# Input rows in their own buffer, five unequal loads, and low parts of the values spread over two row tiles

## The reference

```
scores = where(adj > 0, x @ weight @ input.T, -2**32 + 1)       # 6144 x 6144
atten  = softmax(scores / 0.07, axis=1)
x      = layernorm(x + atten @ input)
# second layer
Wh     = x @ W ;  s1 = Wh @ a1 ;  s2 = Wh @ a2
e      = leaky_relu(s1[:, None] + s2[None, :], 0.2)
att    = softmax(where(adj > 0, e, -9e15), axis=1)
out    = layernorm(x + elu(att @ Wh))
```

## Time and profile before

| | us |
|---|---|
| median of 3 runs | 1605.18 |
| lowest and highest | 1605.13, 1605.41 |
| profiled execution | 1605.25 |
| its span in the trace | 1603.3 |

### The profile page before, as it was taken

The page is one execution under the profiler, slowest core; times in us unless marked ns, Lnnn a source line. Parts: engine busy times, 40 slices in busy tenths (PEclk is TensorE's granted clock), DMA queues, the critical chain, the costliest instruction groups (busy, mean ns, idle before and its releaser), DMA issues.

```text
span 1603.3 us, 29354 instructions
## 1 busy us (share of the span) xinstructions
PE 1520.6 (95%) x10380; PEld 1088.5 (68%) x10380; DVE 1393.5 (87%) x2425; ACT 1061.9 (66%) x2396; POOL 833.3 (52%) x550
## 2 busy tenths in 40 slices
PE   7799999999999999999999999959999999999993
PEld 3577777777777777777777777755665656565652
DVE  6999999999999999999999999957778787888872
ACT  3577777777777777777777777766544444344433
POOL 5343333444343343344433433318988887878784
PEclk9999999999999999999999999989999999999997
DMA  7655555556555555555555555343344333434310
GB/s 236 221 176 187 180 186 199 204 204 204 192 193 180 181 183 197 204 205 204 200 188 185 182 181 191 122 81 79 79 79 92 79 76 81 87 79 92 80 33 13
DMA packets 228208, 241.11 MB, mean 150 GB/s; under 512 B 157152, under 2 KB 203488, under 8 KB 228064
## 3 DMA queue, kind: packets, MB, share of 16 engines
q1 hardware_dynamic: 228064, 239.25, 48.1%
HBM read 160.56 MB, written 40.89 MB: 126 GB/s over the span
## 4 chain that ended last, share of the span: by engine, by line
PE 85%; POOL 4%; issue 3%; DVE 3%; ACT 2%; POOLq 0%; ACTq 0%; DVEq 0%
PE ps L494 16%; PE ps L470 15%; PE ps L558 11%; PE ps L551 8%; PE ps L472 8%; PE ps L507 7%; PE ps L506 7%; PE ps L505 7%; PE ps L535 4%; POOL p_lo L396 2%; DVE p L866 1%; POOL m_w L401 1%; PE ps L567 1%; ACT p_hi L680 1%; DVE ve L907 1%
## 5 line engine op out<-in xcount | busy, mean ns | idle before, releaser
L645 ACT CAST pT_hi<-ps 128x512 f16<-128x512 f32 x576 | 335.8, 583 | 176.3 <-PE ps L494 173.1
L651 ACT ACTIVATE rows<-rows,exp_bias 128x512 f32<-128x512 f32 x576 | 417.9, 725 | 38.5 <-DVE exp_bias L841 38.5
L470 PE MATMUL ps<-vals,pT_hi 128*128 128x256 f16 x2304 | 442.0, 273 | 0.9 <-ACT att L639 0.8
L349 POOL TENSOR_SCALAR edges<-neg_mask 128x1536 uint8<-128x1536 bf16 x192 | 284.3, 1481 | 294.2 <-DVE neg_mask L755 290.3
L866 DVE SCALAR_TENSOR_TENSOR p<-ps,e_col,edgesT 128x1024 f32<-128x1024 f32 x288 | 353.9, 1277 | 87.7 <-POOL p_lo L396 50.4
L396 POOL TENSOR_TENSOR p_lo<-p,p_hi 128x1024 fp32r<-128x1024 f32 x156 | 369.6, 2382 | 80.2 <-PE ps L535 59.9
L472 PE MATMUL ps<-vals,pT_lo 128*128 128x128 f16 x2304 | 411.2, 219 | 0.0
L778 DVE CUSTOM_DVE_ANT_0 rows<-ps,neg_mask 128x1024 f32<-128x1024 f32 x288 | 351.8, 1222 | 52.5 <-PE ps L507 48.7
L787 DVE TENSOR_TENSOR pT_lo<-ps,pT_hi 128x512 f16<-128x512 f32 x576 | 389.3, 683 | 6.5 <-ACT pT_hi L645 6.4
L494 PE MATMUL ps<-ident,rows 128*128 128x128 f32 x2304 | 350.9, 275 | 3.4 <-DVE pT_lo L787 3.2
L680 ACT CAST p_hi<-p 128x1024 fp32r<-128x1024 f32 x156 | 162.9, 1048 | 245.8 <-DVE p L866 241.5
(11 more groups left out here) (99 smaller groups left out, 1323.9 us busy)
## 6 DMA issues: line engine op xcount, KB each, us to landing
adj_sb<-adj SPq DMA_DIRECT2D x192, 768.0 KB, 6.2
edge_rows<-edges SPq DMA_DIRECT2D x192, 192.0 KB, 5.1
rows<-inp SPq DMA_DIRECT2D x4, 768.0 KB, 9.6
xq<-x SPq DMA_DIRECT2D x48, 64.0 KB, 2.0
xr<-x SPq DMA_DIRECT2D x48, 64.0 KB, 1.8
out<-y_w SPq DMA_DIRECT2D x6, 512.0 KB, 3.6
edgesT<-edge_rows SPq DMA_TRANSPOSE x48, 5.3
x_all<-w SPq DMA_DIRECT2D x1, 64.0 KB, 1.8
```

What stands on the lines that cost most here:

```text
L470: nc.tensor.matmul(acc, pT_hi[:, s, cols], vals[:, jb, :], start=(jb == 0), stop=False, skip_group_check=True)
L645: nc.scalar.copy(pT_hi[:, bc % PT_SLOTS, :], ps[:, PT0 + bc % NPT, :]).then_inc(pT_hi_set, 1)
L651: nc.scalar.activation(row_chunk(1 - par, c), row_chunk(1 - par, c), ACT.Exp, bias=exp_bias[:, 1 - par:2 - par], scale=EXP_SCALE, accum_ou ...
```

## The change

It has four parts.

- The input rows get a buffer of their own, `inp_sb`, of 24 KB in each partition. `rows` holds masked scores and turned input chunks only.
- They are loaded in five transfers of 4, 8, 12, 12 and 12 row blocks. The load of x stands behind the first of them, and each later one is followed by a quarter of the adjacency. GpSimd's high parts follow the same five pieces.
- `vals_low` leaves its place in steps 0 to 11 of tile 0, and with it goes the wait of VectorE on itself. Chunks 0 to 3 are made in tile 0 after the mask of steps 5, 7, 9 and 11, and chunks 4 to 11 in tile 1 after the mask of steps 0 to 7.
- TensorE's one wait for all low parts ahead of tile 1's scores goes. In its place each of the 12 `attend` calls of tile 0's probabilities waits for its own chunk.

```diff
+INP_CHUNKS = (1, 2, 3, 3, 3)
...
+        inp_sb = sb0("inp_sb", [P, NB, P], F32)
         rows = sb0("rows", [P, 2 * N], F32)
...
-            for q in range(QUARTERS):
-                b = NB // QUARTERS
-                dst = rows[:, q * b * P:(q + 1) * b * P].rearrange("p (b d) -> p b d", d=P)
-                sp.dma_start(dst, inp_rows[:, q * b:(q + 1) * b, :]).then_inc(inp_in[q], 16)
-                if q == 0:
+            for i in range(len(INP_CHUNKS)):
+                blocks = inp_blocks(i)
+                sp.dma_start(inp_sb[:, blocks, :], inp_rows[:, blocks, :]).then_inc(inp_in[i], 16)
+                if i == 0:
                     sp.dma_start(xq[:], pair_rows(x, 0)).then_inc(xq_in, 16)
+                    continue
+                q = i - 1
                 sp.dma_start(adj_sb[:, q, :], pair_rows(adj, 0)[:, q * QW:(q + 1) * QW]).then_inc(adj_in[q], 16)
...
             def turn_inp(c):
-                pe.wait_ge(inp_in[c // QC], 16)
+                pe.wait_ge(inp_in[piece_of(c)], 16)
...
             def attend(t_of, bc):
                 n = C * t_of + bc
+                if t_of == 0:
+                    pe.wait_ge(vals_lo, bc + 1)
                 pe.wait_ge(pT_lo_set, n + 1)
...
-                    if known == 1 and c == 0:
-                        pe.wait_ge(vals_lo, C)
...
             def vals_low(c):
                 b = slice(c * BPC, (c + 1) * BPC)
-                dve.wait_ge(vals_hi, c // QC + 1)
-                nc.vector.scalar_tensor_tensor(out=vals[:, b, P:2 * P], in0=inp_v[:, b, :], scalar=SPLIT_SCALE,
+                dve.wait_ge(vals_hi, piece_of(c) + 1)
+                nc.vector.scalar_tensor_tensor(out=vals[:, b, P:2 * P], in0=inp_sb[:, b, :], scalar=SPLIT_SCALE,
...
                     if known == 0:
                         if c + Z_LEAD < C:
                             z_low(c + Z_LEAD)
-                        vals_low(c)
-                        dve.wait_ge(vals_lo, c + 1)
...
                         if c in (4, 10) and (known is None or known < NB - 1):
                             make_mask(t + 1, c // 10, None)
+                    if t == 0 and c >= 5 and c % 2 == 1:
+                        vals_low((c - 5) // 2)
+                    if t == 1 and c < 8:
+                        vals_low(c + 4)
```

More of the change, by code:

```diff
@@ L181, in build @@
         weights_in = sem("weights_in")
-        inp_in = [sem(f"inp_in{q}") for q in range(QUARTERS)]
+        inp_in = [sem(f"inp_in{i}") for i in range(len(INP_CHUNKS))]
         adj_in = [sem(f"adj_in{q}") for q in range(QUARTERS)]
@@ L263, in ends_tile, with inp_blocks, piece_of @@
             return known is None or known >= 2
+        def inp_blocks(i):
+            return slice(BPC * sum(INP_CHUNKS[:i]), BPC * sum(INP_CHUNKS[:i + 1]))
+        def piece_of(c):
+            return next(i for i in range(len(INP_CHUNKS)) if c < sum(INP_CHUNKS[:i + 1]))
         block = ctx.enter_context(nc.Block())
@@ L335, in _ @@
                                     pattern=[[-1, P]], channel_multiplier=1).then_inc(ident_set, 1)
[L338 to L343, removed]
+            for i in range(len(INP_CHUNKS)):
+                pool.wait_ge(inp_in[i], 16)
+                nc.gpsimd.tensor_scalar(vals[:, inp_blocks(i), 0:P], inp_sb[:, inp_blocks(i), :], SPLIT_SCALE, None,
+                                        ALU.mult).then_inc(vals_hi, 1)
             def make_edges(t, q):
@@ L442, in turn_inp @@
                     mm = nc.tensor.transpose(ps[:, PT0 + c % 2, b * P:(b + 1) * P],
-                                             rows[:, (c * BPC + b) * P:(c * BPC + b + 1) * P], ident[:])
+                                             inp_sb[:, c * BPC + b, :], ident[:])
                 mm.then_inc(inp_turned, 1)
@@ L728, in _ @@
             nc.vector.tensor_copy(wa_rep[:].rearrange("p a d -> p (a d)"), ps[:, PV, 0:2 * P]).then_inc(wa_copied, 1)
-            inp_v = rows[:, 0:N].rearrange("p (b d) -> p b d", d=P)
             def z_low(c):
```

## The result

The changed kernel takes 1599.14 us (median of 6 runs, 1598.48 to 1600.38), the kernel before 1605.16 us in the same comparison (6 runs). The ratio is 0.9963, 95% interval 0.995 to 0.9976. It is faster by 0.37%, and the whole interval lies beyond the 0.2% that the prediction took as the least that a measurement here can tell from none. The forecast was 1600.7 us with a range of 1598.4 to 1603.8.

What follows compares the result with a forecast made beforehand. TensorE's unbroken run was taken as the bound, so only earlier entry saves time. Step 9 of tile 1 moves from 64.6 to 60.1 us with the lower clock: 1605.25 - 4.5 = 1600.7 us, range 1598.4 to 1603.8.

Steps and rivals of the forecast that it cites:

- What bounds: TensorE, busy 1005.5 of 1008 us from 58 to 1066 us; the saving is how much earlier it enters that run.
- Smaller first transfer: At the start, x and the first four blocks land sooner; bounds 0 to 0.5 us, taken as 0.
- The first mask gets ahead: In tile 0, the first mask starts before GpSimd's conversion; part of the "more than said" rival.
- The wait on itself: VectorE's wait behind each of 12 low parts of the values goes, 0.11 us each: 1.3 us of VectorE.
- Collisions: Low parts beside GpSimd stood still 6.0 us; in new places mostly first behind a mask, 0 taken per pair.
- The walk: VectorE's prices added from 18.40 us: bias 42.7, chunk 0 50.6, chunk 4 58.7, step 9 of tile 1 58.9.
- The clock: TensorE's granted clock falls between 41 and 50.75 us; step 9 at 60.1, gain 4.5 instead of 5.7 us.
- The run from there unchanged in length: Sign to look for: TensorE's run from step 9 of tile 1 to the second layer keeps its length.
- A held clock: Rival: TensorE's clock does not fall ahead of step 9; gain 5.7 us, 1599.5 us, chance 0.28.
- GpSimd gets the port behind each mask: Rival: five low parts wait up to 1.47 us each; gain 0.4, 1604.9 us; chance 0.19 with half-way cases.
- The buffer's place: Rival "slower": moved buffers slow VectorE's reads and writes; at 6.4% slower 1608.2 us, chance 0.05.
- more than said: Rival: first mask ahead of GpSimd or milder tile 0 collisions; gain up to 7.5 us, 1597.8 us, chance 0.06.

Runs made afterwards that it cites:

- e4_four_loads: The changed kernel with four equal input loads of 12 row blocks in place of five; 1598.4 us, ratio to before 0.9959.
- e2_no_self_wait: e1_buffer_loads without VectorE's wait on itself behind each low part; 1602.85 us, ratio to before 0.9991.
- e9_longer_gap: e6_gpsimd_first with a 128x512 copy out of PSUM between mask and low part in place of 128x128; 1603.16 us, ratio to before 0.9989.
- e3_own_waits: e2_no_self_wait with TensorE's one wait for all low parts replaced by one per chunk; 1602.93 us, ratio to before 0.999.
- e1_buffer_loads: The kernel before with only the input buffer of its own and the five loads; 1605.12 us, ratio to before 1.0004.
- e5_clock_held: The changed kernel with 56 extra unused matmuls in TensorE's gaps, tile 0 step 11 to tile 1 step 4; 1597.56 us, ratio to before 0.9957.
- e7_early: The changed kernel with low parts 0 to 2 made at the start, 3 and 4 in tile 0 steps 7 and 9, 5 to 11 in tile 1; 1597.11 us.
- e8: e7_early with the extra matmuls of e5_clock_held; 1596.95 us, ratio to before 0.9951.
- e6_gpsimd_first: The changed kernel with the low parts of tile 1 steps 0 and 2 moved behind a 128x128 copy out of PSUM; 1600.73 us, ratio to before 0.9977.

## Why the prediction was right

- *What bounds.* Right. TensorE is busy 1006.2 of the 1008 us after 52 us (52 to 1060), and nearly all of the gain is made before that run. Its first 3 us are at the low clock:

```profile
52.00:1060.00 1008.00, 1006.18 (x8622) 771.39 (x8620) 943.49 (x1888) 792.91 (x1998) 382.75 (x325) 1.00 0.56 187
```

- *Smaller first transfer, 0.* Right, shown by e4_four_loads. The first mask was held up by GpSimd as before (3.26 us from 15.61, to 18.87; before to 18.48). "The first mask gets ahead" came true in e2_no_self_wait and e9_longer_gap, and was worth nothing there. In e9_longer_gap the mask of step 2 met GpSimd instead (2.97 us at 20.18), and the bias came at 42.08, among the 41.89 to 42.54 of the others.
- *The wait on itself, 1.3 us.* Measured 1.12 from z to the bias, e3_own_waits against e1_buffer_loads.
- *Collisions.* Behind the four later masks VectorE went first (0.67 or 0.68 us each), as taken. In step 5 of tile 0, the one left open between 30.5 and 31.9, GpSimd got in between and the low part ended at 31.78. All 12 stood still for 1.3 us instead of 6.0. One reading behind this was too broad. The low part at 18.99 ended at 22.08, but the conversion of values beside it, from 18.18 on, only at 22.42. So "stands still while a GpSimd instruction that started earlier runs" holds for conversions of masks. Beside this one the low part was done 0.3 us ahead of it, and no run was made to show why.
- *The walk.* It starts at 18.40, and in the profile of the changed kernel the same place, z, is at 18.79. So its landmarks are nearer than its sums. The bias was made at 42.69 (42.7 forecast), but that is 23.9 us behind z and not 24.3. The mask of step 0 ended at 44.58 (44.6). The first `pT_lo` was made at 50.25 (50.6), 31.5 us behind z and not 32.2. That of chunk 2 came at 54.76 (55.0) and that of chunk 4 at 59.46 instead of 58.7. The exact hit at the bias is luck. Of the 0.7 us that the walk is too long, 0.3 lie in step 11 of tile 0, and 0.2 in the low part that meets a conversion, which lost 0.12 us (0.80 for 0.68) and not 0.35. For chunk 4 the walk left out that VectorE's masked sum of step 7 waits for TensorE's scores, and those were late by the low clock (with the clock held, in e5_clock_held, it does not wait):

```profile
57.63 1.23 DVE L781 CUSTOM_DVE_ANT_0 rows<-ps,neg_mask 128x1024 f32<-128x1024 f32 x1 [0.60 <-PE ps L514]
```

  That cost nothing at step 9, which stands 1.75 us behind step 8, TensorE's own pace.
- *The clock.* It fell and cost 1.18 us by e5_clock_held, where 1.2 was worked out. The forecast of which branch it would be was a judgement from one gap, and the reasoning does not say why a gap of 3.2 us was enough here and one of 2.3 us before was not.
- *Gain.* 4.9 us at step 9 against 4.5, but 5.3 us counted from z (46.24 to 40.94). So the walk was 0.8 us too long at step 9, and 0.4 of that was hidden by the later start.
- *What was missed.* "The run from there unchanged in length" is off by 0.6 us: 997.94 from step 9 to the end before, 997.36 after. It was 998.00 in e1_buffer_loads, and 997.25 to 997.38 in e2 to e5, e7 and e8. It is not spread out. Before, the turn at 158.09 is followed by the next 2.03 us later, and in the changed kernel the same two are 1.75 us apart (153.19 and 154.94). Another 0.3 us stands at 979 to 983 us. The kernels that still have VectorE's twelve waits on itself, before and e1_buffer_loads, have both places, and no other kernel has. e6_gpsimd_first and e9_longer_gap (998.47 and 998.39) have further ones, three of about 0.26 us and a few smaller, and the two have them at the same turns though their step 9 is 3.2 us apart. So the places go with the program and not with when the run starts. No experiment was aimed at this, and its cause is open.
- *The sum.* 5.3 us from z and 0.6 in the run are 5.9, against 6.0 between the medians. The profiled executions lie only 5.2 us apart, since in them the changed kernel started 0.4 us later and took 0.3 us more in the second layer. The measured time lies inside the range because the two things that were missed, 0.8 and 0.6 us, are small. Both point the same way.

The rivals. A held clock would have given 58.24 at step 9, shown by e5_clock_held. "GpSimd gets the port behind each mask" was wrong for four of the five places and right for the fifth. With two of the places forced (e9_longer_gap), step 5 comes 3.0 us later behind the bias and step 9 3.3, and the median is 1603.16. That is not the price of the rival alone: 1.2 us are the two copies, and the run behind step 9 is 1.0 us longer than in the changed kernel. The buffer's place changed no duration (e1_buffer_loads). The mild case of "more than said" needed other places for the low parts (e7_early).

## What to carry to other kernels

A wait in the view of waits is worth what is late next. 4.2 us of TensorE waiting for the last low part gave nothing, since VectorE was late for everything behind it as well. New places for that engine's low parts gave 4.2 us. They did it in two ways at once: five low parts stand past the point where the long run starts, and all twelve stand still for less. No run separates the two.

Walk through the slower engine's list with start-to-start prices from the trace, including who holds the shared port. The landmarks came out within 0.8 us. Count from a landmark behind the first loads, since what lies ahead of it scattered by 0.9 us between profiles.

An instruction with all operands in SBUF went well directly behind the one that GpSimd waits for, or in a wait of its own engine, and badly a few tenths later. The exception is a place where GpSimd still has earlier work waiting.

## What the runs showed of the hardware

- A VectorE instruction with two SBUF inputs that starts 0.37 us after a GpSimd conversion of a mask is held to its end (1.65 instead of 0.68 us), and one that starts 0.04 us before it costs GpSimd 0.5 us instead (1.97 for 1.47). Two starts 0.4 us apart thus decide who loses 0.5 or 1 us. Where GpSimd is already waiting, it goes first even between two back-to-back VectorE instructions (0.96 and 1.94 us at 28.95 and 29.84).
- 56 matmuls for nobody, 6.8 us of TensorE in gaps, hold the granted clock at 1.00 and give 1.18 us back from step 5 to step 9. Before the change the same low clock cost nothing, as far as the trace tells: VectorE had no gap up to 58 us, and TensorE waited 2.3 us for it at the end. No run held the clock there.
- A wait of VectorE on its own last instruction costs 0.11 us from start to start, and taking twelve of them away gave 1.12 us.
- Kernels with the same instructions up to the bias reach it at 41.89 to 42.54 us, and all of that scatter lies ahead of z. From there four of them take 23.75 us to the hundredth.
